# A decoder layer on one core: the rank counting of the expert routing moved ahead of a wait, and the routing's bias moved into the mix

## The reference, cut to what matters

```
x = x + attn(layernorm(x))     # delta rule in chunks, two FIR filters, a gate that mixes four parts
x = x + xattn(layernorm(x))    # cross-attention on 64 context rows, 16 heads
x = x + ffn(layernorm(x))      # 8 experts of which each row takes the 2 with the highest score, and a shared one

# attn, its end
wgt = softmax(gelu(gate_in @ fg_w1.T + fg_b1) @ fg_w2.T + fg_b2, over 4), floored and normalized again
o = wgt[0] * short + wgt[1] * long_ + wgt[2] * delta + wgt[3] * v
o = o * rsqrt(mean(o * o over a head) + 1e-05) * o_norm_w ; return o @ o_proj_w.T

# ffn, its routing
scores = sigmoid(xf @ gate_w.T + lb_bias)
topw, topi = top_k(scores, 2)
```

## Time and profile before

| | us |
|---|---|
| runs of the kernel before, three | 1284.79, 1286.12, 1286.15 (median 1286.12) |
| the profiled execution's own time | 1290.98 |
| its span in the profile | 1289.2 |
| PE busy | 1113.9 (86%) |
| DVE busy | 866.2 (67%) |
| POOL busy | 565.6 (44%) |
| ACT busy | 514.2 (40%) |

### The profile page before, as it was taken

How to read it: one execution, slowest core, us unless ns; L and a number is a source line. 1 busy time by engine, 2 the same in 40 slices (tenths; PEclk the granted TensorE clock), 3 DMA queues, 4 the chain that set the end, 5 groups by cost and what they waited for, 6 DMA issues and landing times.

```text
span 1289.2 us, 22573 instructions
## 1 busy us (share of the span) xinstructions
PE 1113.9 (86%) x7730; PEld 852.5 (66%) x7730; DVE 866.2 (67%) x2270; ACT 514.2 (40%) x936; POOL 565.6 (44%) x1003
## 2 busy tenths in 40 slices
PE   3979879697799999899899899899989969886882
PEld 2646458576676767777676687686777758765772
DVE  4898977754767666865766776676687555644467
ACT  4766754315014323512521531432341436633551
POOL 4242426165037437536544634833750243435442
PEclk9999999798899999999999999999999989987996
DMA  6544350611001301300210220130120442323479
GB/s 165 176 132 141 113 199 9 205 67 66 17 1 59 120 1 42 115 18 30 101 49 4 79 91 1 58 120 1 43 73 9 159 169 83 95 70 115 134 233 329
DMA packets 77823, 119.01 MB, mean 92 GB/s; under 512 B 28304, under 2 KB 53392, under 8 KB 75536
## 3 DMA queue, kind: packets, MB, share of 16 engines
q1 hardware_dynamic: 70128, 96.78, 23.2%
q0 software_dynamic: 7584, 20.80, 4.5%
HBM read 66.47 MB, written 51.09 MB: 91 GB/s over the span
## 4 chain that ended last, share of the span: by engine, by line
PE 56%; DVE 25%; issue 6%; ACT 4%; POOL 3%; another core or an unknown queue 2%; DMA 2%; SPq 1%; ACTq 0%; DVEq 0%; POOLq 0%
PE bank L673 7%; DVE arena L1531 5%; PE bank L578 5%; PE bank L558 4%; PE bank L726 4%; PE bank L505 3%; PE bank L885 3%; PE bank L736 2%; PE bank L644 2%; PE bank L545 2%; PE bank L776 2%; PE bank L568 2%; PE bank L892 2%; PE bank L653 2%
## 5 line engine op out<-in xcount | busy, mean ns | idle before, releaser
L957 ACT ACTIVATE arena<-bank 128x512 f32<-128x512 f32 (+1 forms) x326 | 171.5, 545 | 472.5 <-PE bank L568 142.5
L1464 POOL DMA_INDIRECT results<-arena x78 | 76.3, 978 | 105.5 <-DVE arena L2079 75.4
L1531 DVE SCALAR_TENSOR_TENSOR arena<-arena,param 128x512 f32<-128x512 f32 x144 | 106.0, 750 | 23.1 <-ACT arena L980 19.7
L1400 POOL TENSOR_TENSOR arena<-arena 128x126 f32<-128x126 f32 (+22 forms) x217 | 89.8, 414 | 37.6 <-DVE arena L1631 22.1
L673 PEld LDWEIGHTS bank<-arena 128*128 128x128 f32 x768 | 93.1, 200 | 6.8 <-issue 6.7
L1384 POOL COPY arena<-arena 32x128 f32<-32x128 f32 x128 | 51.6, 403 | 104.5 <-DVE arena L1621 98.6
L673 PE MATMUL bank<-arena 128*128 128x128 f32 x768 | 94.0, 283 | 0.0
L1402 POOL TENSOR_TENSOR arena<-arena 128x126 f32<-128x126 f32 (+22 forms) x217 | 85.1, 392 | 17.0
L885 PE MATMUL bank<-arena 128*128 128x128 f32 x624 | 89.4, 290 | 0.5 <-issue 0.3
L1336 POOL DMA_INDIRECT slots_x<-arena x64 | 63.6, 993 | 49.8 <-DVE arena L1823 32.5
L885 PEld LDWEIGHTS bank<-arena 128*128 128x128 f32 x624 | 82.8, 206 | 1.8 <-issue 1.7
(11 more groups left out here) (269 smaller groups left out, 2697.1 us busy)
## 6 DMA issues: line engine op xcount, KB each, us to landing
arena<-slots_x SPq DMA_DIRECT2D x78, 129.0 KB
xt<-x_in SPq DMA_DIRECT2D x16, 512.0 KB, 5.0
kq_T<-kq SPq DMA_DIRECT2D x8, 1024.0 KB, 3.8
kq<-kq_T SPq DMA_DIRECT2D x8, 1024.0 KB, 5.7
arena<-results SPq DMA_DIRECT2D x32, 256.0 KB
arena<-ffn_in SPq DMA_DIRECT2D x7, 768.0 KB, 4.2
vT<-v_T SPq DMA_DIRECT2D x8, 514.0 KB
v_T<-vT SPq DMA_DIRECT2D x8, 512.0 KB, 4.2
```

The lines of the kernel that those rows point to most:

```text
L957: free(act.activation(out_, in_, func, **kw), name)
L1400: own.link(pool.tensor_tensor(tmp, rows32[:, m0:, k].unsqueeze(2).broadcast_to([P, nm, k]), units[:, 0:k, k].unsqueeze(1).broadcast_to([P, ...
L1464: pool.indirect_dma_start(results[:, :], bass.IndirectOffsetOnAxis(ap=dest[:, n % YS:n % YS + 1], axis=0), ys[:, n % YS, :], None).then_in ...
L1531: ins = V.scalar_tensor_tensor(cv[:, k % 4, :], pre[:, j, d:d + GT], param[:, at + d:at + d + 1], cv[:, k % 4, :], ALU.mult, ALU.add)
```

## The change

`ranks` is cut in two: `ranks` keeps the wait for the sigmoid and the five comparing instructions, `chosen` gets the six small ones. In the tail of bodies 1 to 7 `ranks` now stands right behind L2028, ahead of `front_compact` and its wait; `chosen` stays behind `late_added`. The addition of the bias, `routing()`, moves from in front of the mix to behind its first half. In the final stage both functions are called one after the other, where `ranks` stood. No instruction is added or removed, and no other engine's program changes.

```diff
--- before.py
+++ after.py
@@ -1787,6 +1787,9 @@
                 link(V.tensor_tensor(flat, flat, cst("before").unsqueeze(1).broadcast_to([P, T, E * E]), ALU.mult))
                 link(V.tensor_tensor(above, above, equal, ALU.add))
                 link(V.tensor_reduce(rank[:, i * T:(i + 1) * T, :], above, AX.X, ALU.add))
+
+            def chosen(i):
+
                 step(V.tensor_scalar(sel, rank[:, i * T:(i + 1) * T, :], 2.0, None, ALU.is_lt))
                 if i != FIRST[PART[i]]:
                     link(V.tensor_copy(prefix[:, 0, :], prefix[:, T, :]))
@@ -1993,8 +1996,6 @@
                 done(V.tensor_tensor(gw[:, 6, :, :], gw[:, 5, :, :],
                                      gs[:, 2, :].unsqueeze(2).broadcast_to([P, T, 4]), ALU.mult), "gate_ready")
                 dve.wait_ge(sem("gate_ready"), 2 * i + 2)
-                if x:
-                    routing()
                 for t0 in range(0, T, 2):
                     tt = (t0, t0 + 1)
                     ks = {}
@@ -2013,6 +2014,8 @@
                         last = V.scalar_tensor_tensor(om[:, t, :], kvi[:, t, 256:512], gw[:, 6, t, 3:4],
                                                       om[:, t, :], ALU.mult, ALU.add)
                     done(last, "mix_ready")
+                    if x and t0 == 0:
+                        routing()
                 for k in range(2):
                     dve.wait_ge(sem("osq_ready"), 2 * i + k + 1)
                     sums = gw[:, 7, 2 * k:2 * k + 2, :].rearrange("p a b -> p (a b)")
@@ -2028,11 +2031,13 @@
                     ins = V.tensor_tensor(omv, omv, orn[:, k * HT // 2:(k + 1) * HT // 2].unsqueeze(2)
                                           .broadcast_to([P, HT // 2, DH]), ALU.mult)
                 done(ins, "on_ready")
+                if x:
+                    ranks(i - 1)
                 if x and ahead:
                     front_compact(i + 1)
                 if x:
                     late_added()
-                    ranks(i - 1)
+                    chosen(i - 1)
                 dve.wait_ge(sem(f"x{i % G}_loaded"), 16 * (NG // G + i // G + 1))
                 for k in range(2):
                     n = f"oproj{k}.{i}"
@@ -2169,6 +2174,7 @@
             routing()
             steps(1)
             ranks(NG - 1)
+            chosen(NG - 1)
             slots(NG - 1)
             late()
             tiles(PARTS - 1, lambda: steps(1))
```

## The result

The changed kernel takes **1277.1 us** (1276.6 to 1277.9, four runs); the kernel before took 1286.1 beside it (1284.8 to 1286.8, four runs). The ratio is 0.992, with an interval from 0.991 to 0.994: 9.0 us faster (8.1 to 12.1 by the interval), against 6.6 forecast. The profiled execution's own time is 1277.4, its span 1275.0.

A forecast was written before the change was run, and what follows sets the result against it. PE holds 56% of the chain; its touchable wait is L644's 9.8 us for DVE's tail. Tails 7.3 - 6 x 0.05, final stage + 0.7 = 7.7, cut to 6.6 for the clock: 1279.5 us, range 1275.0 to 1284.0.

The forecast's parts named there:

- What bounds the tail: Before L644: DVE's tail is last by less than one microsecond, ACT's blocks second, hanging on `front_compact`, so on POOL.
- 7.3 us for the six tails less 0.3: L644 starts 0.83 to 1.59 us earlier per tail, together 7.3, less 6 x 0.05 for a later `front_compact`.
- bias: Tail: adding the bias behind the mix's first half lets POOL end 0.47 us earlier, all of it reaching `front_compact`.
- contention: Gap before `front_compact`: ranks and POOL slow each other, 0.4 us for POOL and 0.5 for DVE.
- The nearest row: L2028 beside POOL's L1402: 0.33 us of delay for 0.81 us of DVE work, suggesting 0.7 for the ranks; 0.4 taken.
- The rule of the Trainium skill: Two-input VectorE and GpSimd instructions take turns at a shared SBUF port; at strongest, `front_compact` 1.2 us later; rival's chance 0.12.
- Covers costed at nothing: Tail: the later bias delays neither ACT's sigmoid nor PE's fourth product of L611; losing PE's cover costs up to 2.6 us.
- The 1.4 us of cover of DVE behind ACT's blocks: Before L644: DVE's L1769, `chosen` and half of L2041 end some 1.4 us before ACT's 4.34 us of copies.
- 0.7 us in the final stage: Body 7: ranks fill DVE's wait for PE, so `positions` (L633) loses its 0.73 us wait and starts 0.7 us earlier.
- Half off for the clock: Reduced clock in three profiled tails, 2.1 us of the sum; plain runs may have less, so 7.7 becomes 6.6 us.
- The total: Whole kernel: 6.6 us faster, 1286.1 to 1279.5 us.
- The slower rival: L644: shifted pauses lower PE's granted clock, 2.15 us each; +3 us for five tails, +5 for six; chance 0.04.

The follow-up runs named there:

- fill_tt: `bias_only` plus a copy of the ranks' five instructions (four with two SBUF operands) in the gap, results unused; ratio 0.9992 to the kernel before.
- fill_reduce: `bias_only` plus five extra sums of 128x256, one SBUF operand each, in the gap, results unused; ratio 0.9998 to the kernel before.
- both_gap: The changed kernel with `chosen`, the six small instructions, also in the gap ahead of `front_compact`; ratio 0.9998 to the kernel before.
- bias_only: The kernel before with only the bias moved behind the mix's first half, ranks left behind `late_added`; ratio 0.9977 to the kernel before.

## Why the prediction was right, and where its terms were off

- **What bounds the tail.** Right: DVE's last additions, by less than a microsecond in three of the six tails and by 1.6 in the other three, then ACT's blocks. After the change the releaser is L1052 in all six.
- **7.3 us for the six tails less 0.3.** 7.0 forecast, 6.8 in the profiles. That `front_compact` would hardly move was right, but in part by luck: the *bias* was put at 0.47 us there, and alone it gave 0.19. The mix does start 0.58 us earlier (forecast 0.57), but it then meets POOL's steps at other moments: from L2006 to L2022 it takes 5.70 us in body 2 and 6.06 in body 4 of the changed kernel, with the bias in it. Where it takes 5.70 the sums are 0.55 us earlier against the gate, and POOL starts its power only 0.37 earlier, since its wait of 0.76 us has shrunk to 0.08: there POOL itself was the last, against the forecast that all of it reaches `front_compact`. The *contention* was put at 0.4 us for POOL and 0.5 for DVE; it is 0.33 and 0.21. The nearest row, L2028 with its 0.33 us for one instruction, was indeed not typical of shorter ones.
- **The rule of the Trainium skill** ("SBUF — State Buffer", "Who interferes with whom"): it names an instruction of VectorE with two SBUF inputs as what disturbs GpSimd and one with a single SBUF input as what doesn't, and `fill_tt` against `fill_reduce` agrees; at its strongest, a block for the whole instruction, it would have been 1.7 us a tail, and 0.33 was measured.
- **Covers costed at nothing.** PE's L611 and ACT's sigmoid were not delayed by the later bias. The 1.4 us of cover of DVE behind ACT's blocks is 1.4 us (the last addition's first half ends near 528.05, ACT at 529.43).
- **0.7 us in the final stage.** This is the term that was furthest off. At `positions` it was 1.4: the removed wait gave its 0.7, and the earlier mix moved PE's late products by another 0.5, which I had left out. Behind `positions` came more that the sum had at nothing: 2.7 us at the first work for the experts and 4.1 at the routing product of group 7.
- **Half off for the clock.** I took the three reduced tails of the profile for more than a plain run has, and reduced 7.7 to 6.6. No run bears this out: the profiles lose 2.2 us there, and the plain runs of before gave back 2.6 with the pauses filled (0.9 to 4.3), the whole rather than half, though a half isn't excluded.
- **The total.** 6.8 in the tails, 0.1 behind them and 4.1 from body 7 on make 11.0 us in the profiles; the runs say 9.0, with 8.1 to 12.1 possible. The forecast of 6.6 was low by the final stage first and by the half taken off second. How the remaining 2 us between the profiles and the runs divide stays open.
- **The slower rival**, a fall of the clock at L644, was a real mechanism: it came in `both_gap`, `bias_only`, `fill_reduce` and `fill_tt`, 1.6 us each time, not 2.15. The pause of the changed kernel is 1.4 us there, and behind a pause that short no run shows a fall.

## What to carry to other kernels

An idle gap of one engine is a place for work only up to what its partner in the gap can bear: here 2.3 us of work went into 2.2 us and pushed the end back by 0.4, while the small instructions on top (1.0 us, and 1.5 in the gap) cost the whole gain. In this gap five sums with one SBUF operand cost GpSimd's chain nothing that the profile shows, and four instructions with two cost it 0.33 us, a fifth of the worst case. Look at what a pause of PE does to the clock of what stands behind it: shortening a pause that nobody needs can be worth something too. And follow a change past the stage in which it was made: the last body and the final stage gave over a third of what the profiles show.

## What was not expected of the hardware

- The granted clock of TensorE fell behind some pauses of PE and not behind others of the same length. Of the 132 pauses in front of L623 and L644 in the tails of bodies 1 to 6 of the eleven profiles without extra products, 37 were 1.88 to 2.56 us long, and behind 15 of these it fell (mean 0.52 to 0.70 over the work behind the pause, so in part at the lower of the two levels of 1.2 and 2.4 GHz): L644 took 5.4 us instead of 3.8. Behind the other 95, at most 1.87 us long, it never did.
- More work made a kernel faster: 1.9 us of unused products in each pause, 0.2% off the time.
- A copy of 128x8 numbers on DVE took 0.66 us while POOL cleared its blocks, and 0.16 elsewhere.
- The two chains of DVE and POOL fall into fixed patterns: in its two profiles `front_compact` of the changed kernel stands 14.38 to 14.41 or 14.57 to 14.59 us behind the gate, nowhere between.
